# A matmul's own signal, or a drain behind it, at the end of a group in three stages of a graph kernel

## The reference

```
def _gcn_conv(x, W, b, src, dst, norm, num_nodes):
    h = x @ W
    msg = h[src] * norm[:, None]
    out = jax.ops.segment_sum(msg, dst, num_segments=num_nodes)
    return out + b
```

## Time and profile before

| what | us |
|---|---|
| median of 3 executions | 11146.52 (11133.48 to 11153.25) |
| span of the profiled execution | 11128.9 |
| PE busy | 5442.4 (49%) |
| DVE busy | 5035.5 (45%) |
| POOL busy | 6206.8 (56%) |
| ACT busy | 2416.1 (22%) |

### The profile page before, as it was taken

How to read it: one execution, slowest core, us unless ns; L and a number is a source line. 1 busy time by engine, 2 the same in 40 slices (tenths; PEclk the granted TensorE clock), 3 DMA queues, 4 the chain that set the end, 5 groups by cost and what they waited for, 6 DMA issues and landing times. The chain is left out here.

```text
span 11128.9 us, 139837 instructions
## 1 busy us (share of the span) xinstructions
PE 5442.4 (49%) x33091; PEld 4544.5 (41%) x33091; DVE 5035.5 (45%) x16176; ACT 2416.1 (22%) x7480; POOL 6206.8 (56%) x6393
## 2 busy tenths in 40 slices
PE   5333275766751005545555888884333333333333
PEld 3111164666740003334444688883333323332333
DVE  7333475444520006555556677774333333333333
ACT  0000011333310000245555577771000000000000
POOL 3666503654557771056664466664666566656665
PEclk8555577888975555866766999996555555555555
DMA  1000001211100000022222899992111111111112
GB/s 32 2 3 2 5 32 48 44 42 36 40 15 4 2 2 12 12 57 45 45 45 52 297 330 329 330 330 80 47 46 46 51 46 46 46 52 45 46 46 51
DMA packets 387376, 789.79 MB, mean 71 GB/s; under 512 B 162523, under 2 KB 199197, under 8 KB 386574
## 3 DMA queue, kind: packets, MB, share of 16 engines
q0 software_dynamic: 296832, 702.37, 21.8%
q1 hardware_dynamic: 89806, 81.61, 2.2%
q10 hardware_dynamic: 320, 0.80, 0.0%
HBM read 717.69 MB, written 66.66 MB: 70 GB/s over the span
## 5 line engine op out<-in xcount | busy, mean ns | idle before, releaser
L2063 POOL DMA_INDIRECT edge_rows<-tab,all_slots x2352 | 2225.5, 946 | 1321.0 <-issue 670.7
L2120 PE MATMUL edge_psum<-edge_rows,edge_onehot 128*128 x4992 | 1212.0, 419 | 2215.7 <-DVE edge_onehot L2090 1689.0
L2120 PEld LDWEIGHTS edge_psum<-edge_rows,edge_onehot 128*128 128x128 f32 x4992 | 1045.6, 310 | 2382.1 <-issue 2382.1
L2100 DVE TENSOR_TENSOR acc_acc<-acc_acc,edge_psum 128x128 f32 x2496 | 716.4, 287 | 2275.5 <-remote 595.5
L182 POOL DMA_INDIRECT edge_rows<-tab,edge_slots x832 | 814.4, 979 | 992.1 <-DMA edge_slots<-slots_s 547.4
L1868 PE MATMUL edge_p_m<-edge_rows,edge_onehot 128*128 128x128 f32 x9984 | 1172.6, 278 | 176.6 <-DVE edge_rows L1835 108.8
L1868 PEld LDWEIGHTS edge_p_m<-edge_rows,edge_onehot 128*128 128x128 f32 x9984 | 1133.7, 192 | 215.5 <-issue 180.1
L923 POOL DMA_INDIRECT all_x<-tab_src,all_slots x784 | 747.6, 954 | 848.0 <-issue 480.0
L182 POOL DMA_INDIRECT edge_rows<-tab,acc_pair_src x832 | 843.8, 1014 | 671.7 <-remote 274.9
L533 POOL DMA_INDIRECT slots_d<-all_slots,pro_row_d x782 | 756.1, 967 | 565.0 <-DVE pro_row_d L647 328.2
L1800 ACT ACTIVATE edge_rows<-edge_rows,edge_coef 128x128 f32<-128x128 f32 x3328 | 995.1, 387 | 346.5 <-DMA edge_rows<-tab,acc_pair_src 307.7
(11 more groups left out here) (411 smaller groups left out, 10238.9 us busy)
## 6 DMA issues: line engine op xcount, KB each, us to landing
edge_rows<-tab,all_slots POOLq DMA_INDIRECT x2352
tab<-tab_o SPq DMA_DIRECT2D x50, 512.0 KB, 2.6
edge_rows<-tab,edge_slots POOLq DMA_INDIRECT x832
edge_rows<-tab,acc_pair_src POOLq DMA_INDIRECT x832
tab_src<-all_x SPq DMA_DIRECT2D x50, 260.0 KB, 2.1
all_x<-tab_src,all_slots POOLq DMA_INDIRECT x784
slots_d<-all_slots,pro_row_d POOLq DMA_INDIRECT x782
slots_s<-acc_pays,acc_row_s POOLq DMA_INDIRECT x782
```

The lines of the kernel that those rows point to most:

```text
L2063: pool.indirect_dma_start(out=rows[:, (g % R3) * G + j, :], out_offset=None, in_=D[f"tab3_{layer}"][:, :], in_offset=bass.IndirectOffsetOn ...
L2100: v.tensor_tensor(at, at, psum[:, slot % 2, j * P:(j + 1) * P], ALU.add).then_inc(q["added"], 1)
L2120: m = pe.matmul(psum[:, slot % 2, j * P:(j + 1) * P], onehot[:, slot % 2, j, :], flat(rows[:, ds(values[j], 1), :]), start=True, stop=True)
```

## The change

In three places the last matmul of a group no longer raises the semaphore; PE gets a `drain` behind it, and the drain raises it. In `Ranking.slots` the `nop` that raises `used` stays, behind the drain. Nothing else differs: the same matmuls, waits and counts.

```
--- before.py
+++ after.py
@@ Ranking.slots
-            m = pe.matmul(bank, self.K["before_b"][:, :], self.hot_of(KG + k, first, count), start=False, stop=True)
-        m.then_inc(self.ranked, 1)
+            pe.matmul(bank, self.K["before_b"][:, :], self.hot_of(KG + k, first, count), start=False, stop=True)
+        pe.drain(fusable=False).then_inc(self.ranked, 1)
         pe.nop().then_inc(self.used, 1)
@@ relation_rows
-                    m = pe.matmul(p_r[:, slot, j * P:(j + 1) * P], rel[:, t:t + 1].to_broadcast([P, RELS]), K["ident_b"][:, :],
-                                  start=True, stop=True)
-                m.then_inc(q["rel_row"], 1)
+                    pe.matmul(p_r[:, slot, j * P:(j + 1) * P], rel[:, t:t + 1].to_broadcast([P, RELS]), K["ident_b"][:, :],
+                              start=True, stop=True)
+                pe.drain(fusable=False).then_inc(q["rel_row"], 1)
@@ relation_coefs
-                    m = pe.matmul(p_c[:, slot, j * n:(j + 1) * n], relhot[:, slot, j, :], pieces[:, :, :].rearrange("r b k -> r (b k)"),
-                                  start=True, stop=True)
-                m.then_inc(q["coef_sum"], 1)
+                    pe.matmul(p_c[:, slot, j * n:(j + 1) * n], relhot[:, slot, j, :], pieces[:, :, :].rearrange("r b k -> r (b k)"),
+                              start=True, stop=True)
+                pe.drain(fusable=False).then_inc(q["coef_sum"], 1)
@@ edges3, products
-                    m = pe.matmul(psum[:, slot % 2, j * P:(j + 1) * P], onehot[:, slot % 2, j, :], flat(rows[:, ds(values[j], 1), :]), start=True, stop=True)
-                m.then_inc(q["product"], 1)
+                    pe.matmul(psum[:, slot % 2, j * P:(j + 1) * P], onehot[:, slot % 2, j, :], flat(rows[:, ds(values[j], 1), :]), start=True, stop=True)
+                pe.drain(fusable=False).then_inc(q["product"], 1)
```

## The result

The changed kernel takes 11310.53 us (median of 4 runs, 11276.2 to 11340.91), the kernel before 11145.61 beside it (4 runs, 11133.48 to 11153.25): ratio 1.0158, 95% interval 1.0141 to 1.0175. It is slower by 1.6%, where I had forecast 10260 us and put the range's upper end at 11160. The profiled execution has a span of 11274.4 us, 145.5 more than before; it is the fastest of the four.

A forecast was written before the change was run, and what follows sets the result against it. The prediction took waits for PE's late signals beside POOL's indirect DMAs to bound the kernel. 11128.9 - 300 - 270 - 330 + 10 = 10239; with 17.6 us from span to median 10257, say 10260 us, range 9850 to 11160.

The forecast's parts named there:

- What bounds the kernel: Whole kernel: no engine over 56% busy; PE's matmul signals come some 10 us late while POOL issues indirect DMAs.
- The price of a signal by drain: All three places: a drain's signal comes about 0.1 us behind the last matmul; upper bound 7 to 10 us.
- What the drains cost: Ranking, coefficient pass, layer 3: 1432 drains at 0.2 us would be 286 us, mostly covered; 10 us taken.
- The gains of 300, 270 and 330 us: Time saved by prompt signals in the ranking (300), the coefficients (270) and layer 3 (330).
- Rival A: All three places: the drain's message is as late as the matmul's, nothing moves, 11147 us; chance 0.10.
- Rival B: Convolutions and first ranking: the drain is held, and PE with it; 900 and 363 us more, about 12400; chance 0.18.
- point of decision: Rival B's threshold in the convolutions: it decides once drains there last over 1.5 us on average.

## Why the prediction was wrong

**What bounds the kernel**: right. The late signals beside POOL's indirect DMAs were real, and with the scatter gone the coefficient pass takes 235 us (I had worked out 266).

**The price of a signal by drain**: wrong, and the step that failed. I wrote that "what is late seems to be the matmul's message and not the matmul". From the earlier trace rows I had read that the array was free, because the relation rows started 0.2 us behind the coefficients. But the start of a matmul shows that it was issued, not that the one before was finished, and its length isn't measured. The Trainium skill, "Perfetto Trace Analysis", section "Summary: the profiler window per engine type", lists TensorE's end as an estimate and leaves the semaphore out of the window. This case agrees: drains of up to 20.6 us stand behind products shown with 2.07. The runs showed instead that the work itself is finished late, at 2.8 us for a weight load and matmul. A drain waits for just that. The rule of the Trainium skill, "PSUM — Partial Sum Buffer", section "Engine vs sequencer instructions", which I weighed and set aside, held in both halves in the coefficient pass: DVE waits 10.46 us for the matmul's signal in the earlier trace rows and 10.46 for the drain's after.

One reading of rows was wrong too, without bearing on the step: the additions at 8504.45 in the earlier trace rows aren't those of the products at 8494.52. PE was a group ahead; they belong to the group whose products end at 8490.46, so that signal was 14.0 us late and not 7.9.

**What the drains cost**: wrong by place, not by price alone. With POOL silent they cost 0.05 us each, below the 0.2 I took. Beside POOL they cost about 0.6% in the rankings and 0.5% in layer 3, and about nothing in the coefficient pass. I had PE held by the drain itself only; that its sequencer's next load would also have to wait, 1.1 us a group when PE catches up, I had not seen.

**The gains of 300, 270 and 330 us**: all three hung on the failed step; none came.

**Rival A** had the mechanism of the signal, and fits the coefficient pass to 0.1%. **Rival B** had the side: the drain is held, and PE with it, in convolutions and first ranking. Its prices were far too high: 363 us for a ranking that lost 50, and 900 for a layer that lost 76. The error there was to let a third of the groups that PE's lead had spared pay a delay of full length, while the traces show hardly more long waits in the ranking (83 for 74) and fewer in layer 3 (239 for 270). Its point of decision, drains of over 1.5 us on average, was passed: they average 3.75 us in layer 3 (median 1.70), 2.1 of them beyond the products. So it named the side and not the size.

**Still open**: what of POOL's DMA issue PE and DVE contend for; why layer 2 is spared; how much of layer 3's loss is the uncovered register load and how much the lower clock; why in the ranking the drain's signal costs more than the matmul's with a bare drain behind it; and whether a deliberate pause of POOL would pay, which wasn't tried.

## What to carry to other kernels

A matmul's start in a trace shows that it was issued and its end is computed, so before changing who raises a late signal, find out whether the work is late: vary the number of instructions ahead of the signal, or put matmuls that wait for nothing behind it and look at their starts. Beside a stream of indirect DMAs, cut instructions ahead of the signals that matter (0.9976, 0.996 to 0.9991, for one matmul in place of four), and look at the whole loop, since the next engine in it may crawl instead. A drain in front of an engine's next work gives up that engine's lead, and whatever its sequencer has to do for the next group then comes uncovered behind it: put such loads ahead of the drain, which wasn't tried here.

## What the hardware showed unexpectedly

- Beside POOL's scatters (one per 1.27 us) PE finishes a weight load and a matmul in 2.8 us, with POOL silent in some 0.1. Beside its gathers filler matmuls start every 0.7 or 1.4 us, though only in stretches, and a pause of POOL ends 63 of 70 of them.
- DVE's chain of additions pays the same 2.8 us an addition where PE's share is small.
- Behind a drain PE's next products start 1.4 us after the last ones, where a wait for the same signal leaves 0.25: 1.0 us of it is a register load that otherwise runs under the matmuls.
- Letting POOL wait for the landing of the DMA two before (in layer 3 of the group two before) made the kernel faster by 0.4% (0.9936 to 0.9986) and left the delays as they were.
